# A perceiver layer on one core: order of keys and values, mask sign and reciprocals' rows in the first stage

## What is computed

```python
# 1 cross attention, 16 heads of 16, additive mask (batch, query, context row)
q, k, v = norm(x) @ Wq.T + bq, ctx @ Wk.T + bk, ctx @ Wv.T + bv
scores = q k^T / 4 + mask;  out = softmax(scores) v @ Wo.T + bo
# 2 a Mamba-2 block of which only batch 0's Y is used, divided by a norm:
A = A_param * softplus(norm(x) @ W_dt + dt_bias); cumA = cumsum(A)
out = Y[0] / (exp(cumA) * cumsum(exp(-cumA))) @ W_out.T
# 3 a mixture of 8 experts, the best 2 per token, weighted by a softmax of 2
out = sum_e gate_e * (silu(x @ w_gate_e) * (x @ w_up_e)) @ w_down_e
```

## Time and profile before

| | |
|---|---|
| median of 3 runs | 1574.52 us (1573.39 to 1575.89) |
| profiled execution | 1575.44 us, its span 1573.4 us |
| busy share of the span | PE 93%, PEld 83%, DVE 69%, ACT 60%, POOL 58% |
| granted TensorE clock, mean | 0.968 of full speed |
| start of the first scores / last batch's end / first expert product | 22.77 / 982.2 / 1035.28 us |

### The profile page before, as it was taken

The page is one execution under the profiler, slowest core; times in us unless marked ns, Lnnn a source line. Parts: engine busy times, 40 slices in busy tenths (PEclk is TensorE's granted clock), DMA queues, the critical chain, the costliest instruction groups (busy, mean ns, idle before and its releaser), DMA issues. The chain is left out here.

```text
span 1573.4 us, 52396 instructions
## 1 busy us (share of the span) xinstructions
PE 1463.1 (93%) x15242; PEld 1306.0 (83%) x15243; DVE 1093.2 (69%) x3895; ACT 951.7 (60%) x2387; POOL 918.4 (58%) x1505
## 2 busy tenths in 40 slices
PE   6979999999999999999999998569999999999997
PEld 6858888888888888888888887359999999999996
DVE  3647777777777777777777777446767766766664
ACT  4716666666666666666666666046666666666663
POOL 4616666666666666666666665236555566565563
PEclk9969999999999999999999999579999999999999
DMA  5302533433322322222222221412222222222222
GB/s 179 80 11 73 155 101 108 152 102 109 79 65 72 79 65 72 78 65 72 78 65 73 78 65 36 172 36 37 37 33 37 37 35 35 37 34 36 37 34 27
DMA packets 81413, 109.05 MB, mean 69 GB/s; under 512 B 17104, under 2 KB 59088, under 8 KB 81200
## 3 DMA queue, kind: packets, MB, share of 16 engines
q1 hardware_dynamic: 65680, 89.63, 20.1%
q0 software_dynamic: 15680, 18.76, 7.7%
HBM read 90.50 MB, written 18.55 MB: 69 GB/s over the span
## 5 line engine op out<-in xcount | busy, mean ns | idle before, releaser
L697 ACT ACTIVATE wd<-wd,nmx 128x257 f32<-128x257 f32 x512 | 254.8, 500 | 88.3 <-DVE nmx L833 84.7
L833 DVE CUSTOM_DVE_ANT_0 wd<-sc,wd 128x257 f32<-128x257 f32 x512 | 188.6, 423 | 65.3 <-PE sc L375 57.9
L1550 POOL DMA_INDIRECT out<-par,oi x71 | 112.9, 1590 | 169.2 <-ACT par L1456 165.8
L1351 PE MATMUL y_p<-wd,hT 128*128 x852 | 195.5, 379 | 0.7 <-DVE hT L1511 0.7
L1485 DVE TENSOR_TENSOR gw_lo<-wg,gw_hi 128x1408 fp32r<-128x1408 f32 x71 | 115.4, 1625 | 115.4 <-ACT gw_hi L1429 115.4
L1202 POOL TENSOR_TENSOR ctx_lo<-wd,ctx_hi 128x516 fp32r<-128x516 f32 x128 | 165.2, 1291 | 49.0 <-ACT ctx_hi L673 45.6
L434 PE MATMUL pt<-con,wd 128*128 128x128 f32 x1024 | 163.6, 283 | 27.0 <-ACT wd L673 24.9
L1351 PEld LDWEIGHTS y_p<-wd,hT 128*128 128x128 f32 x852 | 159.5, 190 | 19.2 <-issue 0.9
L375 PE MATMUL k<-ctx_hi,wkh 128*128 128x256 f32 x512 | 159.1, 311 | 0.6 <-POOL ctx_lo L1202 0.6
L375 PE MATMUL v_p<-wvh,ctx_hi 128*128 128x256 f32 x512 | 158.2, 309 | 0.5 <-ACT y L673 0.5
L673 ACT ACTIVATE wd<-pt 128x512 f32<-128x512 f32 x256 | 151.6, 592 | 2.5 <-PE pt L434 1.8
(11 more groups left out here) (191 smaller groups left out, 4319.8 us busy)
## 6 DMA issues: line engine op xcount, KB each, us to landing
wd<-in_ctx SPq DMA_DIRECT2D x128, 258.0 KB, 2.7
wd<-in_mask SPq DMA_DIRECT2D x512, 32.1 KB, 1.7
wd<-in_wd SPq DMA_DIRECT2D x8, 768.0 KB, 9.6
wg<-in_wg SPq DMA_DIRECT2D x8, 704.0 KB
wu<-in_wu SPq DMA_DIRECT2D x8, 704.0 KB
wd<-in_x SPq DMA_DIRECT2D x32, 128.0 KB, 2.1
xr<-in_x SPq DMA_DIRECT2D x32, 128.0 KB, 2.1
out<-x SPq DMA_DIRECT2D x32, 128.0 KB, 1.8
```

The costliest lines, as they stand in the source:

```text
L697: nc.scalar.activation(pr[:, g, :], sm[:, g, :], ACT.Exp, bias=nmx[:, g:g + 1], scale=-1.0, accum_out=rsum[:, g:g + 1]).then_inc(exp_done, 1)
L833: V.tensor_tensor_reduce(sm[:, g, :], SC[g][:, 0:S], msk[:, b, :], 1.0, 3.0e38, ALU.add, ALU.min, nmx[:, g:g + 1]).then_inc(max_done, 1)
L1351: return nc.tensor.matmul(out, lhsT, rhs, start=start, stop=stop)
L1550: G.indirect_dma_start(outd[:, :], bass.IndirectOffsetOnAxis(oi[:, s, 1:2].bitcast(U32), 0), yb[:, s, :], None, compute_op=ALU.add).then_i ...
```

## The change

TensorE's step becomes scores, turn_c of the step before, keys, values, turn_a, first transposes, weighting, turn_b, second transposes. ScalarE takes the values and splits the context before it copies the first probabilities; copies of transposes and the decays move between the first exponential and the others of the step that follows. On VectorE `residual1` and `statistics2` move from the end of b0 behind the maxima of b1, the rest of softplus ahead of `take_output`, and `reciprocals` ahead of it too. The mask stays as it is: the queries are scaled by +1/4 and the instruction of the maxima multiplies by -1. `rp` gets 128 partitions, of which 32 are written and the others zeroed once; `expand` multiplies over all 128.

```diff
-        rp = sb("rp", [2 * H, P])
+        rp = sb("rp", [P, P])
@@ TensorE: expand
-                        last = mm(M[:, o:o + P], cst(e)[0:2 * H, a * P:(a + 1) * P], rp[:, :])
+                        last = mm(M[:, o:o + P], cst(e)[:, a * P:(a + 1) * P], rp[:, :])
@@ TensorE: tile
                     if runs(nxt[0]):
                         scores(*nxt)
+                    turn_c(*((i, b - 1) if b else (i - 1, TB - 1)))
                     if runs(two[0]):
                         project_k(*two)
+                        project_v(*two)
                     turn_a(i, b)
+                    if runs(nxt[0]):
+                        transpose_probs(*nxt, 0)
                     if runs(i):
                         weigh_values(i, b)
-                    if runs(nxt[0]):
-                        transpose_probs(*nxt, 0)
                     turn_b(i, b)
-                    if runs(two[0]):
-                        project_v(*two)
                     if runs(nxt[0]):
                         transpose_probs(*nxt, 1)
-                    turn_c(i, b)
@@ TensorE: before the tiles
+            pe.wait_ge(blank_rows, 1)
...
             project_k(0, 1)
+            project_v(0, 1)
             transpose_probs(0, 0, 0)
-            project_v(0, 1)
             transpose_probs(0, 0, 1)
@@ ScalarE: take_rp
+                act.wait_ge(blank_rows, 1)
...
-                copy(rp[:, b * Q:(b + 1) * Q], RP).then_inc(rp_done, 1)
+                copy(rp[0:2 * H, b * Q:(b + 1) * Q], RP).then_inc(rp_done, 1)
@@ ScalarE: tile
+                    if runs(nxt[0]):
+                        exponentials(*nxt, 0)
+                    if b == 0 and runs(i - 2):
+                        decays(i - 2)
+                    if b == 2 and runs(i - 1):
+                        take_z2T(i - 1)
+                    if b == 3 and runs(i - 2):
+                        take_z3T(i - 2)
+                    if runs(nxt[0]):
+                        exponentials(*nxt, 1, 2, 3)
+                    if runs(two[0]):
+                        take_values(*two)
+                    if b == 1 and runs(i - 2):
+                        take_ynT(i - 2)
                     if runs(three[0]):
                         split_high(*three)
                     if runs(nxt[0]):
-                        exponentials(*nxt, 0, 1, 2)
-                    if b == 1 and runs(i - 2):
-                        take_ynT(i - 2)
-                    if runs(nxt[0]):
-                        exponentials(*nxt, 3)
+                        take_probs(*nxt, 0)
                     if runs(i):
                         take_rp(i, b)
-                    if runs(nxt[0]):
-                        take_probs(*nxt, 0)
...
-                    if runs(two[0]):
-                        take_values(*two)
                     if runs(nxt[0]):
                         take_probs(*nxt, 1)
-                    if b == 1 and runs(i - 1):
-                        take_z2T(i - 1)
-                    if b == 2 and runs(i - 2):
-                        take_z3T(i - 2)
-                    if b == 3 and runs(i - 1):
-                        decays(i - 1)
@@ VectorE: maxima
-                        held(dve, (init, 2), (mask_done, n + 1), (exp_done, 4 * n), (s_ready, 4 * n + 1))
+                        held(dve, (init, 2), (msk_in[b], 64 * (i + 1)), (exp_done, 4 * n), (s_ready, 4 * n + 1))
...
-                    V.tensor_tensor_reduce(sm[:, g, :], SC[g][:, 0:S], msk[:, b, :], 1.0, 3.0e38, ALU.add, ALU.min,
+                    V.tensor_tensor_reduce(sm[:, g, :], SC[g][:, 0:S], msk[:, b, :], -1.0, 3.0e38, ALU.add, ALU.min,
@@ VectorE: take_queries
-                    V.tensor_scalar(qs[:, a, :], M2[:, a, :], prm("bq")[:, a:a + 1], -float(HD) ** -0.5,
+                    V.tensor_scalar(qs[:, a, :], M2[:, a, :], prm("bq")[:, a:a + 1], float(HD) ** -0.5,
@@ VectorE: tile
                     if runs(nxt[0]):
-                        maxima(*nxt, 0, 1)
-                    if runs(nxt[0]):
-                        maxima(*nxt, 2, 3)
-                    if b == 0 and runs(i - 1):
-                        weigh(i - 1)
-                    if b == 2 and runs(i + 1):
-                        take_queries(i + 1)
-                    if b == 3 and runs(i - 2):
-                        take_logits(i - 2)
+                        maxima(*nxt, 0, 1, 2, 3)
+                    if b == 1 and runs(i - 1):
+                        residual1(i - 1)
+                        statistics2(i - 1)
                     if runs(two[0]):
                         take_keys(*two)
                     if b == 3 and runs(i - 1):
                         softplus_series(i - 1, 1, len(ATANH))
-                    if runs(i):
-                        take_output(i, b)
+                        softplus_end(i - 1)
                     if b == 0 and runs(i - 1):
+                        weigh(i - 1)
                         attention_out(i - 1)
                     if b == 1 and runs(i - 1):
                         normalise2(i - 1)
                     if b == 2 and runs(i - 2):
                         normalise3(i - 2)
-                    if b == 3 and runs(i - 1):
-                        softplus_end(i - 1)
+                    if b == 2 and runs(i + 1):
+                        take_queries(i + 1)
+                    if b == 3 and runs(i - 2):
+                        take_logits(i - 2)
                     if runs(nxt[0]):
                         reciprocals(*nxt)
+                    if runs(i):
+                        take_output(i, b)
...
-                    if b == 0 and runs(i - 1):
-                        residual1(i - 1)
-                        statistics2(i - 1)
@@ VectorE: before the tiles
+            V.memset(rp[:, :], 0.0).then_inc(blank_rows, 1)
@@ GpSimd: negate_mask and its calls go; tile
+                    if runs(two[0]):
+                        lay_queries(*two)
                     if runs(three[0]):
                         split_low(*three)
-                    if runs(two[0]):
-                        lay_queries(*two)
-                        negate_mask(*two)
```

More of the change, by code:

```diff
@@ L235, in attend @@
         x2_out, blank_out = sem("x2_out"), sem("blank_out")
-        vl_ready, vl_done, last_done, mask_done = sem("vl_ready"), sem("vl_done"), sem("last_done"), sem("mask_done")
+        vl_ready, vl_done, last_done = sem("vl_ready"), sem("vl_done"), sem("last_done")
         k_ready, k_done, v_ready, v_done = sem("k_ready"), sem("k_done"), sem("v_ready"), sem("v_done")
@@ L239, in attend @@
         pt_ready, pt_done = sem("pt_ready"), sem("pt_done")
-        own_done = sem("own_done")
+        own_done, blank_rows = sem("own_done"), sem("blank_rows")
         rec_done, pl_done, px_done = sem("rec_done"), sem("pl_done"), sem("px_done")
@@ L804, in _ @@
             exponentials(0, 0, 0, 1, 2, 3)
+            take_values(0, 1)
             take_probs(0, 0, 0)
-            take_values(0, 1)
             take_probs(0, 0, 1)
@@ L1215, in lay_queries @@
                               ).then_inc(last_done, 1)
-            def negate_mask(i, b):
-                held(pool, (con_in, 16), (msk_in[b], 64 * (i + 1)))
-                G.tensor_scalar(msk[:, b, :], msk[:, b, :], -1.0, None, ALU.mult).then_inc(mask_done, 1)
             def last_probs(i, b):
@@ L1271, in _ @@
             lay_queries(0, 0)
-            negate_mask(0, 0)
             normalise1(1)
@@ L1275, in _ @@
             lay_queries(0, 1)
-            negate_mask(0, 1)
             split_low(0, 2)
```

## The result

The changed kernel takes 1776.0 us, the median of 4 runs (1770.4 to 1780.7), beside 1574.7 us before: a ratio of 1.128, 95% interval 1.124 to 1.131. The forecast was 1557 us, with a range of 1540 to 1590. The time rose where it was to fall, and ends 186 us above the range.

A forecast was written before the change was run, and what follows sets the result against it. TensorE's instruction list was taken to bound the kernel; in the new order a late VectorE and ScalarE chain limits the gain. Tiles of 28.75 us for 29.40, 28 x 0.65 = 18 us off 1575.4, give 1557 us; range 1540 to 1590.

The forecast's parts named there:

- the values' arrival: ScalarE in b3, the tile's fourth batch: values arrive 3.91 us after scores and bind it; 6.5 us with the instruction stream.
- What is late next: Prediction's section on the VectorE and ScalarE chain from b1's scores to b3's: 15.22 us where TensorE alone needs 13.67.
- The slower rival: Late maxima spread into b3 through a ring of three engines: a tile of 29.85 us, 1588 us; chance 0.25.
- The tail of residual2: VectorE's 3.20 us from residual2 to b2's maxima, ending 3.1 us after b2's scores; b2's second transposes wait 1.5 us.
- b0 and b3: Steps of a tile's first and fourth batch, forecast at 7.03 and 6.5 us.
- the same path: In b0, the path from values' arrival through copy, split, probabilities and transposes on ScalarE: 7.03 us for TensorE's 6.98.
- TensorE's own list: TensorE's group prices summed in the new order: 26.94 us a tile for 29.40, 69 us gained if alone; chance 0.13.
- The small edits: Mask and 128-row reciprocals: the expansion on TensorE gains 0.09 us a tile, the mask's negation nothing.
- the edits at nothing: Prediction's section of edits priced at nothing, among them GpSimd losing the mask's negation and the -1 in the maxima.

The follow-up runs named there:

- e1_v4: The changed kernel with four buffers for the values in place of two, orders of all engines untouched: 1613.9 us, ratio 1.024.
- e7_fill: The changed kernel with four unused matmuls a step ahead of TensorE's second transposes: 1714.8 us, ratio 1.089.
- e3_maskrp: The kernel before with only the unnegated mask and the reciprocals on 128 rows: 1562.6 us, ratio 0.992.
- e12_adjweigh: Kernel before with mask and rows edits, ScalarE's reciprocals' copy behind the first probabilities' copy, plus the values' run moved behind the keys': 1676.2 us, ratio 1.065.

## Why the prediction was wrong

**The step that failed** is that in b3 "the values' arrival" (at 3.91 us) "binds ScalarE in any case", and the chain in "What is late next", which puts "the copy of the values 0.50" behind the exponentials with its input as its only condition. Its second condition, the buffer's, stands in the code and in no row of the kernel before, since it was always met there. With it, b3 is not 6.5 but 8.0 us, b0 8.3 for 7.0, b1 8.5 for 7.0, b2 9.1 for 8.2 (without the clock's falls): 33.9 us a tile for 28.75. e1_v4 takes the condition away and gives back 3.2 us of it in every tile. The prediction's own terms would have shown most of this, by an estimate: the weighting of b0 ends 0.62+0.2+1.54+1.42+0.90+0.54+0.62 = 5.84 us after the scores; ScalarE starts the copy 0.18 later (the group behind the weighting starts at 614.14, the copy at 614.32), and then follow 0.50+0.54+0.65+0.54, together 8.25 us for a measured 8.27. For b3 the same gives 5.25+0.18+2.23 = 7.66 for 8.02.

**The clock** was held at full speed in the sum without a word. The waits took it down (mean 0.93 from 150 to 1100 us): 61 us, by e7_fill. The slower rival, too, priced waits at their length.

**The tail of residual2** was right in mechanism and nearly in size. In e1_v4 the way from b1's scores to b3's takes 15.50 us (610.00 to 625.50) for the 15.22 of the sum. b2 takes 8.19 of them; 15.22 less b1's 6.98, 8.24, had been forecast. But TensorE's wait is not where it was put, 1.5 us at the second transposes: it is 0.7 us at the queries, for z2T, and only 0.2 there. The row of VectorE in the changed kernel shows the tail:

```profile
607.12 0.42 DVE L959 TENSOR_TENSOR x<-m,xk 128x256 f32<-128x256 f32 x1 [1.64 <-PE m L375]
...
610.44 0.43 DVE L834 CUSTOM_DVE_ANT_0 wd<-sc,wd 128x257 f32<-128x257 f32 x1 [0.25 <-issue]
```

3.32 us for 3.20, and 2.98 us after b2's scores (607.46) for 3.1.

**b0 and b3** were too short even without the missed wait: 7.9 and 7.3 us in e1_v4 for 7.03 and 6.5. The wait for the reciprocals' copy ahead of b1's scores (0.6 us) is not in b0's sum, and the wait of turn_z1 for the logits (0.7 us), which the change puts behind the whole softplus on VectorE, was not seen at all. Nor can b0's 7.03 be worked out again: "the same path" gives 3.78+0.19+0.50+0.54+0.65+0.54 = 6.20 there, less than TensorE's own 6.98. Against the kernel before with the same mask and rows (29.2 us a tile, the mean b2 6.89) these 30.7 us are 1.5 longer, 1.3 of it in b2.

**TensorE's own list** came out as summed: values at 0.12, expansion 0.89, the first transposes 0.53 to 0.56 ahead of the weighting. That sum said 69 us of gain and was worth nothing, because the values' run was the cover of three latencies (the copy of the first probabilities, z1T's copy, the ranks). The prediction saw it as the cover of residual2's tail alone.

**The small edits** were put at 2.5 us and gave 12 to 13 (e3_maskrp). The entry of the expansion from the keys' run (0.09 us) was left out of the sum, and the negation, which the prediction lists under "the edits at nothing", was worth 7.

**The sum of the 201 us**, from the kernels: the clock's falls 61 (changed less e7_fill); the values' buffer condition 101 (e7_fill less e1_v4); what is left of the new orders 51 (e1_v4 less e3_maskrp, most of it b2); less 12 for the mask and the rows (before less e3_maskrp). The falls of the clock are the condition's too: with it gone, in e1_v4, none is left in the loop.

## What to carry to other kernels

When a step moves on one engine, read every condition of every instruction that is moved or passed, the buffers' above all: a condition that was always met has no row in the profile, and it is the first to bind in a new order. A long run with no dependence on its surroundings, between two dependent short ones, is cover, and joining it with another to save an entry of 0.08 us a step cost 130 us. Price a new wait of TensorE at its length, and allow for a fall of the clock besides (here 1.5 us each): some waits brought one and some did not.

## What the runs showed of the hardware

In the changed kernel the granted clock fell to its lower level again and again with no recurring wait of TensorE above 1.4 us. The length of the longest wait doesn't tell whether it falls: in e1_v4 it held at full speed through the loop with waits of up to 1.0 us, and in e12_adjweigh it fell with none above 0.8. There the same three waits came in two neighbouring tiles, 0.47, 0.84 and 0.54 us within 3 us (to 601.32), after which the clock held, and 0.47, 0.84 and 0.58 (to 633.40), after which it fell. Below is how a fall looks in the changed kernel, b0's keys after waits of 1.16 and 0.23 us: the starts are 0.21 us apart and go back to 0.12 from 628.14 on.

```profile
627.74 0.41 PE L375 MATMUL k<-ctx_lo,wkh 128*128 128x256 f32 x1
627.96 0.35 PE L375 MATMUL k<-ctx_hi,wkl 128*128 128x256 f32 x1
628.14 0.29 PE L375 MATMUL k<-ctx_hi,wkh 128*128 128x256 f32 x1
```

Unused matmuls in place of waiting (e7_fill) kept the clock up and made the kernel 61 us faster.
